# Two attention blocks over 16 images: how queries and keys are stacked and how the row sums become reciprocals

## Chip, cores, metric
One core of one Trainium2 chip. The metric is the device time of the kernel in microseconds, the median of several runs.

## What is computed
Input x is 16 images of 128 channels x 1024 pixels, float32. Each image passes two attention blocks in turn. The reference, cut to what matters:

```python
# block 0: 4 heads of 32 channels
_x = group_norm(x, 32 groups, eps 1e-6) * gn_scale + gn_bias
q, k, v = lin(_x, Wq), lin(_x, Wk), lin(_x, Wv)          # each (16, 4 heads, 32, 1024)
scores  = einsum('bhdxy,bhdij->bhxyij', q, k) / sqrt(128)
weights = softmax(scores, over the 1024 key pixels)
h = lin(einsum('bhxyij,bhdij->bhdxy', weights, v), Wp)
x = (x + h) / sqrt(2)
# block 1: one head of 128 channels
h = group_norm(x, 8 groups, eps 1e-5) * gn_w + gn_b
q, k, v = split(h @ qkv_w.T + qkv_b)
out = softmax(q @ k.T / sqrt(128)) @ v @ proj_w.T + proj_b + x
```

## The kernel before
**Rounds and gaps.** The work on TensorE is written out by hand as tables of pieces. There is a `head`, then 16 rounds (round i is image i's) and a last round that finishes the rest. A round has 64 gaps (`GAPS`), one for each score product of block 0: L828 makes a 128 keys x 512 queries tile of one head, and ScalarE takes its exponential (L553). In the same gap TensorE, ScalarE and VectorE each do the pieces that the tables give for that gap, in the order of the table. A piece is written as (name, argument, image offset, gap on TensorE, gap on ScalarE, gap on VectorE); a gap of 64 or more (`GAPS + n`) is folded into the next round by `folded`. GpSimd and SP don't run by gaps: they have an order of their own and wait on semaphores alone.

**Block 0 in split precision.** q and k are made by `q0` and `k0` (L911). ScalarE writes a rounded high part (`high`, L608), VectorE the rest as a low part (`low`, L702): the tiles q_hi, q_lo, k_hi, k_lo, each 128 channels (4 heads x 32) by 1024 pixels. A score product wants 96 rows to contract for each head: q_stack has hi, lo, hi of the queries in its three groups of 32 partitions, k_stack has hi, hi, lo of the keys. SP makes the stacks: `put_parts` writes the four parts to DRAM (L405), `stack_queries` (L413) and `stack_keys` (L419) read them back with the heads rearranged from partitions to columns. q_stack has three slots of half an image each, k_stack two of a whole image.

**Maxima ahead of the scores.** 64 `max` products for each image (L906, on the same stacks, with VectorE's reduction at L711) find the row maxima for image i+1 during round i. The first and the thirty-third of them wait for the stacks (`stacked_q`, `stacked_k`). A maximum of 16 rows is turned and brought into row 96 of q_stack (`gather`, `shift`, `load_shift` at L425). `MAX_EARLY` and `MAX_LATE` say in which gaps they stand. PSUM has two shared banks for all pieces of this kind, and a third tile, `acc`.

**Sums.** Products with v (`pv`, L846) add into `acc`, whose two halves of an image ScalarE saves to `mix` (`save`). GpSimd adds the probabilities of a half in 14 additions (L517; n counts 28 for a round). `sums` (L929) adds over partitions, ScalarE copies the result to `rb` (L629), where each head's sums stand in all of its 32 partitions. SP then gathers one row of each head into `compact` by four transfers with 32-byte pieces (`turn_sums`, L432), VectorE takes the reciprocal of 64x32 (L735), SP writes it to DRAM (L438), waits, and spreads it to `rb` by four transfers (`spread_reciprocals`, L442). VectorE multiplies `mix` by it (`scale`, L740), and `proj` (L933) follows.

**GpSimd's other work.** `rstd` (L501) for the two norms, after the additions n = 7 and n = 17, and `form_x1` (L506) after n = 21.

**Block 1** runs for image i-1 in eight tiles, eight gaps apart: `score1` (L864 to L866), `max1`, `exp1`, `turn` (L872), `pv1a` and `pv1b` (L885), then `out` (L937). It starts at gap 41 of a round and ends in the next round.

## Time and profile before
| | |
|---|---|
| median of 3 runs | 1848.18 us (1838.9 to 1850.77) |
| the profiled execution | 1824.1 us, its span 1822.1 us |
| TensorE busy | 1641.6 us, 90% |
| VectorE, ScalarE, GpSimd busy | 1133.0, 1076.8, 1096.0 us |
| granted TensorE clock, mean | 0.945 |
| a full round | 105.5 us |

The span runs from the first to the last instruction of the profiled execution. A granted clock of 1.00 is 2.4 GHz and 0.50 is 1.2 GHz.

### The profile page before, as it was taken

What the parts mean: (1) busy time and instruction counts of PE and PEld (TensorE: products, weight loads), DVE (VectorE), ACT (ScalarE), POOL (GpSimd) and SP (SyncE); (2) the same over time, 40 slices, a digit from 0 to 9 for tenths busy, and PEclk for the clock granted to TensorE, in tenths of its full rate; (3) what the DMA queues carried; (4) which work ended last, traced back from release to release, by engine and by line L of the source; (5) the groups of instructions that cost most, each with busy time, mean ns of one, the idle gap of its engine ahead of it and who ended that gap; (6) DMA issues with size and microseconds to landing.
All of it is one profiled execution on the core that took longest, in us unless ns stands there. A gap on an engine that the chain in (4) does not pass through costs nothing.

```text
span 1822.1 us, 25657 instructions
## 1 busy us (share of the span) xinstructions
PE 1641.6 (90%) x9319; PEld 1082.2 (59%) x9319; DVE 1133.0 (62%) x1897; ACT 1076.8 (59%) x1825; POOL 1096.0 (60%) x503
## 2 busy tenths in 40 slices
PE   3889798989989898998989899998989999889978
PEld 1334365656656665665666566665656666556647
DVE  2666575756767675766767566676756666676232
ACT  1245465656656565665656566565656666556734
POOL 1077676665757666575766657477655747765720
PEclk8598899999999999999999999999999999999989
DMA  6131304140321414032140404114040411300000
GB/s 189 58 70 65 76 19 115 38 122 24 100 58 36 117 36 122 24 111 49 35 127 26 122 25 118 46 42 116 25 122 25 124 39 46 101 24 13 13 12 18
DMA packets 65837, 120.63 MB, mean 66 GB/s; under 512 B 26032, under 2 KB 26672, under 8 KB 65712
## 3 DMA queue, kind: packets, MB, share of 16 engines
q1 hardware_dynamic: 65712, 118.99, 23.3%
q8 instruction: 75, 1.23, 0.3%
q14 instruction: 50, 0.41, 0.1%
HBM read 76.22 MB, written 42.21 MB: 65 GB/s over the span
## 4 chain that ended last, share of the span: by engine, by line
PE 72%; DMA 11%; SPq 5%; DVE 5%; issue 3%; ACT 3%; POOL 0%; ACTq 0%; POOLq 0%; DVEq 0%
PE bank L906 13%; PE acc L846 12%; PE scores L885 11%; PE scores L828 10%; DMA k_stack<-parts_dram 9%; PE scores L872 5%; PE acc L911 3%; PE bank L911 3%; PE scores L864 3%; PE scores L865 3%; PE scores L866 3%; DVE halfmax L711 3%; SPq L432 2%; PE bank L933 2%; PE bank L915 2%
## 5 line engine op out<-in xcount | busy, mean ns | idle before, releaser
L517 POOL TENSOR_TENSOR sum<-sum,probs 128x1024 f32<-128x1024 f32 x448 | 1048.7, 2373 | 467.8 <-PE acc L846 425.0
L711 DVE TENSOR_REDUCE halfmax<-bank 128x1 f32<-128x512 f32 x1024 | 679.6, 686 | 363.7 <-PE bank L906 358.1
L553 ACT ACTIVATE probs<-scores 128x512 f32<-128x512 f32 x896 | 519.3, 600 | 458.2 <-PE scores L828 453.5
L906 PE MATMUL bank<-k_stack,q_stack 96*128 96x512 f32 x1024 | 457.3, 465 | 133.1 <-DMA k_stack<-parts_dram 104.7
L828 PE MATMUL scores<-q_stack,k_stack 97*128 97x512 f32 x1024 | 443.9, 446 | 2.3 <-DMA q_stack<-neg 2.3
L906 PEld LDWEIGHTS bank<-k_stack,q_stack 96*128 96x128 f32 x1024 | 198.4, 198 | 302.6 <-issue 179.8
L885 PEld LDWEIGHTS scores<-v,turned 128*128 128x128 f32 x1952 | 253.8, 192 | 36.9 <-ACT turned L573 17.1
L885 PE MATMUL scores<-v,turned 128*128 128x128 f32 x1952 | 260.7, 277 | 4.6 <-ACT turned L573 3.5
L846 PE MATMUL acc<-probs,v 128*32 128x512 f32 x1792 | 236.6, 642 | 0.0
L828 PEld LDWEIGHTS scores<-q_stack,k_stack 97*128 97x128 f32 x1024 | 197.0, 194 | 62.7 <-issue 37.8
L753 DVE TENSOR_REDUCE negmax<-scores 128x1 f32<-128x1024 f32 x128 | 156.5, 1222 | 59.8 <-PE scores L866 59.5
L566 ACT ACTIVATE probs<-scores,negmax 128x1024 f32<-128x1024 f32 x128 | 142.5, 1113 | 24.8 <-DVE negmax L753 24.8
L573 ACT COPY turned<-scores 128x1024 f32<-128x1024 f32 x122 | 123.5, 1012 | 50.3 <-PE scores L872 50.1
L501 POOL TENSOR_TENSOR gn<-gn,minus_half 128x1 f32<-128x1 f32 x32 | 17.6, 550 | 196.7 <-DVE gn L686 196.7
L872 PE MATMUL scores<-consts,probs 128*128 128x128 f32 x1024 | 133.0, 272 | 0.6 <-ACT probs L566 0.4
L872 PEld LDWEIGHTS scores<-consts,probs 128*128 128x128 f32 x1024 | 119.8, 141 | 19.1 <-ACT probs L566 2.0
L846 PEld LDWEIGHTS acc<-probs,v 128*32 128x32 f32 x1792 | 51.1, 116 | 124.5 <-issue 100.1
L553 ACT ACTIVATE sum<-scores 128x512 f32<-128x512 f32 x128 | 73.4, 597 | 76.8 <-PE scores L828 76.7
L864 PE MATMUL scores<-k_hi,q_hi 128*128 128x512 f32 x256 | 107.4, 419 | 3.0 <-DVE k_lo L702 1.8
L865 PE MATMUL scores<-k_lo,q_hi 128*128 128x512 f32 x256 | 104.3, 407 | 0.0
L866 PE MATMUL scores<-k_hi,q_lo 128*128 128x512 f32 x256 | 103.9, 406 | 0.0
L581 ACT ACTIVATE mixed<-scores,rowinv 128x128 f32<-128x128 f32 x128 | 47.1, 368 | 38.0 <-PE scores L885 38.0
(86 smaller groups left out, 1318.9 us busy)
## 6 DMA issues: line engine op xcount, KB each, us to landing
q_stack<-parts_dram SPq DMA_DIRECT2D x96, 256.0 KB, 4.4
k_stack<-parts_dram SPq DMA_DIRECT2D x48, 512.0 KB, 9.4
xin<-x_dram SPq DMA_DIRECT2D x16, 512.0 KB, 3.5
x<-x_dram SPq DMA_DIRECT2D x16, 512.0 KB, 3.6
parts_dram<-q_hi SPq DMA_DIRECT2D x16, 512.0 KB, 2.6
parts_dram<-q_lo SPq DMA_DIRECT2D x16, 512.0 KB, 3.6
parts_dram<-k_hi SPq DMA_DIRECT2D x16, 512.0 KB, 2.6
parts_dram<-k_lo SPq DMA_DIRECT2D x16, 512.0 KB, 3.7
```

The source lines that it names most:

```text
L517: pool.tensor_tensor(total, total, probs[:, ring_slot(i, half, kt), 2 * two:2 * two + 2, :], ALU.add).then_inc(added[two], 1)
L553: act.activation(dst, score_bank(i, index), ACT.Exp).then_inc(exp_done, 1)
L711: dve.tensor_reduce(halfmax[:, h, t, half:half + 1], banks[p][:, :], AX.X, ALU.max).then_inc(bank_free[p][VE], 1)
L753: dve.tensor_reduce(negmax[:, t:t + 1], score1_pair(j, t), AX.X, ALU.max, negate=True).then_inc(negmax_done, 1)
L828: pe.matmul(score_bank(i, index), ks[0:SPLIT + 1, i % 2, h, tile(kt)], qs[0:SPLIT + 1, q_half(i, half), h, :], start=True, stop=True).then ...
L846: mm = pe.matmul(acc[head(h), :], v0[:, i % 2, kt, head(h)], src, start=kt == 0, stop=kt == KT - 1, tile_position=(0, DH * h))
L864: pe.matmul(dst, q_hi[:, tile(t)], k_hi[:, halves(half)], start=True, stop=False)
L865: pe.matmul(dst, q_hi[:, tile(t)], k_lo[:, halves(half)], start=False, stop=False)
L866: pe.matmul(dst, q_lo[:, tile(t)], k_hi[:, halves(half)], start=False, stop=True).then_inc(score1_full, 1)
L872: mm = pe.transpose(score1_pair(j, t)[:, tile(kt)], probs1_of(j, t)[:, tile(kt)], identity)
L885: mm = pe.matmul(out1(j, t), turned_of(j, t)[:, tile(kt)], v1[:, kt, :], start=kt == 0, stop=kt == KT - 1)
L906: mm = pe.matmul(dst[:, :], qs[0:SPLIT, q_half(i, arg // FIRST), h, tile(t % 4)], ks[0:SPLIT, i % 2, h, halves(half)], start=True, stop=True)
```

## The change
1. `put_parts` goes. `stack_queries` copies from the parts in SBUF, for each head and group one transfer of 32 partitions x 512 columns (64 KB), 12 for each half; `stack_keys` likewise, 12 transfers of 32 x 1024 (128 KB). That is 36 transfers an image. They are issued in SP's order where the reading transfers stood; the queries wait for q0 alone, the keys for k0.
2. `turn_sums`, `spread_reciprocals`, `compact` and both DRAM scratch tensors go. VectorE takes the reciprocal of `rb` in place, in four quarters of 128x128 for each half. The multiplication with `mix` goes to GpSimd, after the additions n = 20 (half 0) and n = 2 of the next round (half 1); `form_x1` goes to n = 4, the two `rstd` to n = 6 and n = 20.
3. Pieces stand in other gaps: the first `max` at gap 19 (was 18), the thirty-third at 54 (was 52), the last at 87 as before, with 34 early and 30 late (were 27 and 37); `sums` of half 1 at gap 71 (was 70); the order in which the `max` tiles are taken changes too.

The diff, cut to its core:

```diff
-            ("exp1", t, 0, None, first + 2, None),
+            ("exp1", t, 0, None, first + 1, None),
...
 MAX_EARLY = (
-    18, 24, 26, 28, 29, 30, 31, 32, 33, 35, 49, 50, 51, 51, 52, 54, 56, 57, 58, 61, 62, 65, 66, 67, 68, 78, 87,
+    19, 25, 27, 27, 28, 35, 36, 36, 38, 43, 44, 47, 51, 53, 53, 57, 59, 60, 64, 65, 66, 67, 67, 68, 69, 71, 76, 77,
+    78, 81, 82, 83, 86, 87,
 )
 MAX_LATE = (
-    19, 26, 27, 30, 33, 34, 35, 36, 40, 41, 42, 43, 45, 46, 46, 47, 52, 52, 54, 59, 59, 62, 64, 65, 66, 68, 69, 73,
-    74, 74, 75, 77, 79, 80, 82, 83, 85,
+    19, 24, 25, 28, 29, 30, 31, 31, 33, 34, 41, 44, 45, 47, 48, 50, 51, 54, 55, 59, 60, 62, 62, 67, 68, 69, 73, 73,
+    74, 79,
 )
...
-    ("q0", 0, 2, GAPS + 5, GAPS + 5, GAPS + 6), ("q0", 1, 2, GAPS + 6, GAPS + 6, GAPS + 6),
-    ("k0", 0, 2, GAPS + 6, GAPS + 6, GAPS + 6), ("k0", 1, 2, GAPS + 7, GAPS + 7, GAPS + 7),
-    ("v0", 0, 2, GAPS + 7, GAPS + 8, None), ("v0", 1, 2, GAPS + 16, GAPS + 17, None),
+    ("q0", 0, 2, GAPS + 5, GAPS + 5, GAPS + 5), ("q0", 1, 2, GAPS + 5, GAPS + 5, GAPS + 5),
+    ("k0", 0, 2, GAPS + 6, GAPS + 6, GAPS + 8), ("k0", 1, 2, GAPS + 7, GAPS + 7, GAPS + 8),
+    ("v0", 0, 2, GAPS + 11, GAPS + 11, None), ("v0", 1, 2, GAPS + 20, GAPS + 20, None),
...
-    ("save", 0, 0, None, 35, None), ("sums", 0, 0, 45, 45, None), ("recip", 0, 0, None, None, 51),
-    ("scale", 0, 0, None, None, 59), ("proj", 0, 0, 61, None, 61), ("stats1", 0, 0, None, None, 61),
-    ("save", 1, 0, None, GAPS + 3, None), ("sums", 1, 0, GAPS + 6, GAPS + 6, None),
-    ("recip", 1, 0, None, None, GAPS + 13), ("scale", 1, 0, None, None, GAPS + 19),
-    ("proj", 1, 0, GAPS + 20, None, GAPS + 20), ("stats1", 1, 0, None, None, GAPS + 22),
+    ("save", 0, 0, None, 34, None), ("sums", 0, 0, 45, 45, None), ("recip", (0, 0), 0, None, None, 49),
+    ("recip", (0, 1), 0, None, None, 52), ("recip", (0, 2), 0, None, None, 54), ("recip", (0, 3), 0, None, None, 57),
+    ("proj", 0, 0, 61, None, 61), ("stats1", 0, 0, None, None, 62), ("save", 1, 0, None, GAPS + 2, None),
+    ("sums", 1, 0, GAPS + 7, GAPS + 7, None), ("recip", (1, 0), 0, None, None, GAPS + 10),
+    ("recip", (1, 1), 0, None, None, GAPS + 11), ("recip", (1, 2), 0, None, None, GAPS + 15),
+    ("recip", (1, 3), 0, None, None, GAPS + 15), ("proj", 1, 0, GAPS + 19, None, GAPS + 19),
...
+ADD_THEN = {
+    2: (("scale", 1, -1),), 4: (("form", 0, 0),), 6: (("rstd", 1, -1),), 20: (("rstd", 0, 2), ("scale", 0, 0),),
+}
...
-    ("save", 1, -1, None, 4, None), ("sums", 1, -1, 6, 6, None), ("recip", 1, -1, None, None, 8),
-    ("scale", 1, -1, None, None, 14), ("proj", 1, -1, 15, None, 15), ("stats1", 1, -1, None, None, 15),
+    ("save", 1, -1, None, 4, None), ("sums", 1, -1, 6, 6, None), ("recip", (1, 0), -1, None, None, 7),
+    ("recip", (1, 1), -1, None, None, 7), ("recip", (1, 2), -1, None, None, 7), ("recip", (1, 3), -1, None, None, 7),
+    ("proj", 1, -1, 9, None, 9), ("stats1", 1, -1, None, None, 9),
...
-        STACK_DMAS = 3
+        STACK_DMAS = 3 * HEADS
...
+        def max_of(n):
+            return n // FIRST * 4 + n // 4 % 4, n // 16 % 2, n % 4
...
             def stack_queries(i, half):
-                sp.wait_ge(parts_out, 64 * (i + 1))
+                for piece in [("q0", h, i) for h in range(2)]:
+                    sp.wait_ge(bank_free[bank_of(piece)][VE], given_back(piece))
...
-                for group, k in enumerate((0, 1, 0)):
-                    sp.dma_start(qs[DH * group:DH * (group + 1), q_half(i, half), :, :].bitcast(F32),
-                                 parts_dram[k][:, halves(half)].rearrange("(h r) n -> r h n", h=HEADS)).then_inc(
-                                     stacked_q[half], 16)
+                hi, lo = part[0:2]
+                for h in range(HEADS):
+                    for group, src in enumerate((hi, lo, hi)):
+                        sp.dma_start(qs[DH * group:DH * (group + 1), q_half(i, half), h, :].bitcast(F32),
+                                     src[head(h), halves(half)].bitcast(F32)).then_inc(stacked_q[half], 16)
 
             def stack_keys(i):
-                for group, k in enumerate((2, 2, 3)):
-                    sp.dma_start(ks[DH * group:DH * (group + 1), i % 2, :, :].bitcast(F32),
-                                 parts_dram[k].rearrange("(h r) n -> r h n", h=HEADS)).then_inc(stacked_k, 16)
+                for piece in [("k0", h, i) for h in range(2)]:
+                    sp.wait_ge(bank_free[bank_of(piece)][VE], given_back(piece))
+                hi, lo = part[2:4]
+                for h in range(HEADS):
+                    for group, src in enumerate((hi, hi, lo)):
+                        sp.dma_start(ks[DH * group:DH * (group + 1), i % 2, h, :].bitcast(F32),
+                                     src[head(h), :].bitcast(F32)).then_inc(stacked_k, 16)
...
                 if has0(i + 1):
-                    put_parts(i + 1)
-                if i:
-                    turn_sums(i - 1, 1)
-                if has0(i + 1):
                     stack_queries(i + 1, 0)
                     stack_keys(i + 1)
-                if i:
-                    spread_reciprocals(i - 1, 1)
...
-                turn_sums(i, 0)
-                spread_reciprocals(i, 0)
...
+            def scale(half, i):
+                pool.wait_ge(recip_done, 4 * (2 * i + half + 1))
+                pool.wait_ge(saved, 2 * i + half + 1)
+                pool.tensor_tensor(mix[:, halves(half)], mix[:, halves(half)], rb[:, halves(half)],
+                                   ALU.mult).then_inc(scaled, 1)
...
-            def recip(half, i):
-                dve.wait_ge(sums_in, 16 * HEADS * (2 * i + half + 1))
-                dve.reciprocal(compact[:, half, :], compact[:, half, :]).then_inc(recip_done, 1)
...
+            def recip(half, quarter, i):
+                if quarter == 0:
+                    piece = ("sums", half, i)
+                    dve.wait_ge(bank_free[bank_of(piece)][SC], given_back(piece))
+                cut = rb[:, HALF * half + C * quarter:HALF * half + C * (quarter + 1)]
+                dve.reciprocal(cut, cut).then_inc(recip_done, 1)
```

## Rows read from the trace of the kernel before

**Rows 1.** The page, part 1: busy us, share and instructions of each engine.
```profile
PE 1641.6 (90%) x9319; PEld 1082.2 (59%) x9319; DVE 1133.0 (62%) x1897; ACT 1076.8 (59%) x1825; POOL 1096.0 (60%) x503
```

**Rows 2.** Waits, whole span: who waited for whom, us in total, times, longest.
```profile
PE bank L906 <- DMA k_stack<-parts_dram: 104.7, 16, 15.2
```

**Rows 3.** Timeline of TensorE: start, us, what, count, [idle before <-releaser].
```profile
43.08 1.19 PE L906 MATMUL bank<-k_stack,q_stack 96*128 96x512 f32 x2 [15.20 <-DMA k_stack<-parts_dram]
...
104.70 1.19 PE L906 MATMUL bank<-k_stack,q_stack 96*128 96x512 f32 x2 [3.62 <-DMA k_stack<-parts_dram]
...
713.43 0.39 PE L866 MATMUL scores<-k_hi,q_lo 128*128 128x512 f32 x1
713.66 0.39 PE L828 MATMUL scores<-q_stack,k_stack 97*128 97x512 f32 x1
719.74 0.76 PE L906 MATMUL bank<-k_stack,q_stack 96*128 96x512 f32 x1 [5.69 <-DMA k_stack<-parts_dram]
...
782.67 0.27 PE L924 MATMUL bank<-consts,rowmax 128*16 128x128 f32 x1
...
800.70 1.06 PE L929 MATMUL bank<-sum,ones 128*32 128x512 f32 x8
```

**Rows 4.** Windows: length, busy us of each engine, granted clock, DMA share, GB/s.
```profile
700.00:705.00 5.00, 5.00 (x34) 3.56 (x36) 3.02 (x4) 3.65 (x7) 0.00 (x0) 1.00 0.96 383
...
710.00:714.00 4.00, 4.00 (x27) 3.30 (x25) 2.13 (x3) 2.40 (x5) 4.00 (x2) 1.00 1.05 222
714.10:719.70 5.60, 0.00 (x0) 0.00 (x0) 0.00 (x0) 0.63 (x2) 5.60 (x4) 0.80 0.79 153
719.70:726.00 6.30, 6.26 (x25) 2.98 (x26) 4.87 (x4) 1.69 (x3) 4.16 (x2) 0.64 0.23 83
...
705.50:811.00 105.50, 99.00 (x586) 67.13 (x582) 70.49 (x119) 67.27 (x115) 68.06 (x32) 0.97 0.26 71
```

**Rows 5.** Timeline of SP's queue: start of the issues, us, count.
```profile
23.00 0.33 SPq L405 DMA_DIRECT2D parts_dram<-q_hi  x1
...
698.88 0.33 SPq L405 DMA_DIRECT2D parts_dram<-q_hi  x1
...
702.58 3.34 SPq L432 DMA_DIRECT2D compact<-rb  x4
706.01 1.48 SPq L413 DMA_DIRECT2D q_stack<-parts_dram  x3
...
719.79 1.71 SPq L442 DMA_DIRECT2D rb<-recip_dram  x4
...
1744.28 2.40 SPq L432 DMA_DIRECT2D compact<-rb  x4
```

**Rows 6.** DMA issues: count, KB each, median us from issue to landing.
```profile
k_stack<-parts_dram SPq DMA_DIRECT2D x48, 512.0 KB, 9.4
...
rb<-recip_dram SPq DMA_DIRECT2D x128, 64.0 KB, 2.0
```

**Rows 7.** Groups of instructions: busy us, mean ns | idle before, releaser.
```profile
L517 POOL TENSOR_TENSOR sum<-sum,probs 128x1024 f32<-128x1024 f32 x448 | 1048.7, 2373 | 467.8 <-PE acc L846 425.0 <-ACT probs L553 42.8
...
L740 DVE TENSOR_TENSOR mix<-mix,rb 128x512 f32<-128x512 f32 x32 | 64.9, 2027 | 5.2 <-DMA rb<-recip_dram 5.2
...
L758 DVE RECIPROCAL rowinv<-rowsum 128x1 f32<-128x1 f32 x128 | 19.7, 154 | 23.8 <-ACT probs L566 23.8
...
L735 DVE RECIPROCAL compact<-compact 64x32 f32<-64x32 f32 x32 | 10.8, 339 | 5.2 <-DMA compact<-rb 5.1
```

**Rows 8.** Timeline of GpSimd in one round.
```profile
705.25 16.26 POOL L517 TENSOR_TENSOR sum<-sum,probs 128x1024 f32<-128x1024 f32 x7 [10.21 <-PE acc L846]
...
761.59 9.36 POOL L517 TENSOR_TENSOR sum<-sum,probs 128x1024 f32<-128x1024 f32 x4 [13.98 <-PE acc L846]
...
786.48 14.07 POOL L517 TENSOR_TENSOR sum<-sum,probs 128x1024 f32<-128x1024 f32 x6
```

**Rows 9.** Timeline of the tail, VectorE's multiplication.
```profile
1754.20 0.68 DVE L740 TENSOR_TENSOR mix<-mix,rb 128x512 f32<-128x512 f32 x1
```

More of the change, by code:

```diff
@@ L64 @@
 BLOCK1 = [(p[0], p[1], -1) + p[3:] for t in range(KT) for p in tile_pieces(t, TILE_FIRST + TILE_GAPS * t)] + [
-    ("out", 0, -1, GAPS + 14, None, GAPS + 14), ("out", 1, -1, GAPS + 41, None, GAPS + 41),
+    ("out", 0, -1, GAPS + 13, None, GAPS + 13), ("out", 1, -1, GAPS + 42, None, GAPS + 43),
 ]
@@ L274, in bass_two_attention_blocks @@
         rb = sb("rb", [C, N])
-        compact = sb("compact", [C // 2, 2, HEADS * KT])
         halfmax = sb("halfmax", [C, HEADS, KT, 2])
@@ L426, in load_shift @@
                     "p h (t n) -> p (h t) n", n=C).bitcast(F32), neg[:, :].bitcast(F32)).then_inc(shift_loaded, 16)
-            def turn_sums(i, half):
-                piece = ("sums", half, i)
-                sp.wait_ge(bank_free[bank_of(piece)][SC], given_back(piece))
-                for h in range(HEADS):
-                    sp.dma_start(compact[:, half, KT * h:KT * (h + 1)], rb[DH * h:DH * h + 1, halves(half)].rearrange(
-                        "o (p e) -> o p e", e=KT)).then_inc(sums_in, 16)
-            def spread_reciprocals(i, half):
-                n = 2 * i + half + 1
-                sp.wait_ge(recip_done, n)
-                sp.dma_start(recip_dram[:, halves(half)].rearrange("h (p e) -> p h e", e=KT),
-                             compact[:, half, :].rearrange("p (h e) -> p h e", h=HEADS)).then_inc(recip_out, 16)
-                sp.wait_ge(recip_out, 16 * n)
-                for h in range(HEADS):
-                    sp.dma_start(rb[head(h), halves(half)],
-                                 recip_dram[h:h + 1, halves(half)].to_broadcast([DH, HALF])).then_inc(rb_loaded, 16)
             def store(i, half):
@@ L527, in _ @@
                     add(i, half, kt, two)
-                    if n == 7 and has0(i - 1):
-                        rstd(1, i - 1)
-                    if n == 17 and has0(i + 2):
-                        rstd(0, i + 2)
-                    if n == 21:
-                        form_x1(i)
+                    for piece, arg, offset in ADD_THEN.get(n, ()):
+                        if has0(i + offset):
+                            if piece == "form":
+                                form_x1(i + offset)
+                            elif piece == "scale":
+                                scale(arg, i + offset)
+                            else:
+                                rstd(arg, i + offset)
+            scale(1, images - 1)
             rstd(1, images - 1)
@@ L708, in maximum @@
                 p = bank_of(piece)
-                t, half, h = n // 8, n // 4 % 2, n % 4
+                t, half, h = max_of(n)
                 dve.wait_ge(bank_full[p], filled(piece))
@@ L731, in shift @@
                                   ALU.mult).then_inc(bank_free[p][VE], 1)
-            def recip(half, i):
-                dve.wait_ge(sums_in, 16 * HEADS * (2 * i + half + 1))
-                dve.reciprocal(compact[:, half, :], compact[:, half, :]).then_inc(recip_done, 1)
-            def scale(half, i):
-                dve.wait_ge(rb_loaded, 16 * HEADS * (2 * i + half + 1))
-                dve.wait_ge(saved, 2 * i + half + 1)
-                dve.tensor_tensor(mix[:, halves(half)], mix[:, halves(half)], rb[:, halves(half)],
-                                  ALU.mult).then_inc(scaled, 1)
+            def recip(half, quarter, i):
[4 more added lines that the diff above has]
+                dve.reciprocal(cut, cut).then_inc(recip_done, 1)
             def residual(half, i):
@@ L804, in _ @@
                         elif name == "recip":
-                            recip(arg, img)
-                        elif name == "scale":
-                            scale(arg, img)
+                            recip(*arg, img)
                         elif name == "proj":
@@ L901, in work @@
                 if name == "max":
-                    t, half, h = arg // 8, arg // 4 % 2, arg % 4
+                    t, half, h = max_of(arg)
                     if arg % FIRST == 0:
```

34 lines of the change are left out of this document (10 added, 24 removed).

## Prediction
> **What bounds the kernel now.** I began with the page: TensorE is busy for 1641.6 us, 90% of the span, and VectorE, ScalarE and GpSimd for 59 to 62% [rows 1]. The list of waits then says what ends TensorE's idle time. Inside the rounds it is almost one thing: the `max` product of L906 waits for the stacked keys, 104.7 us in 16 waits, of which the longest (15.2 us) is in the head [rows 2]. The timeline of one round shows the place: TensorE runs the score product of gap 17 and then that of gap 18 at 713.66, and stands until 719.74 [rows 3]. The windows give the price. In 714.1 to 719.7 TensorE does nothing, in 719.7 to 726.0 the granted clock is 0.64 on average (it has fallen to the lower of the two levels, 1.2 GHz, after the idle stretch, and comes back to 2.4 GHz), and of the round's 105.5 us 99.0 are busy [rows 4]. So a round is TensorE's work plus one stall. The stall costs 85.9/14 = 6.1 us by the waits (104.7 less 15.2 and less the 3.6 of the first round [rows 2, 3]) and 6.3 x (1 - 0.64) = 2.3 us of half-speed work: 8.4 us.
>
> Where the keys' time goes is seen on SP's queue [rows 5]: q's parts leave for DRAM at 698.88; at 702.58 four `compact` transfers of the reciprocals take 3.34 us of issue; three query transfers go at 706.01 and take 1.48 us of issue, the three of keys follow and land 9.4 us (median) after their issue [rows 6], the last just before 719.74.
>
> **Removed: the trip through DRAM.** In place of four transfers out, six in and the four `compact` ones between, SP issues 12 for the first half of the queries as soon as both q_lo are there (the 698.88 of today; their new places are at most a gap earlier, which I keep as reserve), then 12 for the keys. Issue: three neighbours took 1.48 us, 0.49 each; four 64 KB ones to 32 partitions took 1.71 us, 0.43 each [rows 5]. 24 x 0.49 = 11.8, so the last is issued by 710.7, and at 2.0 us to landing for a 64 KB one [rows 6] it lands at 712.7. Data: 12 x 64 KB and 12 x 128 KB. When the six DRAM-fed transfers to 32-partition groups ran, the engines were full (share 1.05) at 222 GB/s [rows 4]. At that rate the queries (0.79 MB, 3.5 us) are bound by issue, 5.9 us to 704.8, and the keys (1.57 MB) by data, 7.1 us, landing at 704.8 + 7.1 + 2.0 = 713.9. No SBUF to SBUF transfer of this size is in the trace. One end is 712.7; the other is the worst run of issues from SBUF to SBUF, 3.34/4 = 0.835 us: 698.9 + 20.0 + 2.0 = 720.9. I take 713.9, since both the 64 KB row and the 222 GB/s row have the new destination shape, while the 0.835 is of 32-byte pieces that also waited in a full queue.
>
> The Trainium skill has a rule against this edit: "DMA: Bandwidth & Descriptors", section Rules for kernel authors, says to coalesce many small transfers, and its section Bandwidth gives 138 GB/s at 64 KB; as an estimate by that figure 2.36 MB need 17.1 us, keys would land near 718, and 3 us of stall would stay. Its rule that 32 partitions reach 8 of 16 ports, some 218 GB/s ("SBUF — State Buffer", Door 1), agrees with the 222 measured [rows 4].
>
> **Moved: the first `max`**, from gap 18 to 19. TensorE reaches it after gap 18's score and its three L864 to L866 products. Today's gap 18 score ends at 714.05; the products stand 0.23 us apart [rows 3], so four more slots give 715.0. The rest of the stretch between k0 and this point keeps its load: 9 `max` products before and after, v0's first half moves in and its second out. 713.9 is before 715.0: no stall, and with no idle stretch no fallen clock. The margin is 1.1 us, so I charge 0.5 us per round. What is late next is TensorE's own work: 97.1 us of a round (99.0 - 2.3, and 0.4 of small waits).
> Gain: 14 x 8.4 = 117.6; the first round has 3.6 + 2.3 = 5.9 [rows 3]; less 14 x 0.5 = 7.
>
> The second half's queries are issued when score 31 is read; the first `max` that wants them is at gap 54 (52 before), twenty gaps later. 12 issues (5.9 us) there hide, and the shift's transfer ahead of them stays ahead. In that stretch the queue loses five reciprocal transfers and four spreads, so `load_shift` and the stores come no later.
>
> **Head.** Today q_lo is there at 23.00 [rows 5] and the first `max` runs at 43.08 [rows 3]. The same sum gives 23.0 + 5.9 + 7.1 + 2.0 = 38.0. What follows is paced by VectorE, so 5.1 us are gained whole.
>
> **Reciprocals.** Each half now costs VectorE four of 128x128. 128x1 takes 154 ns, 64x32 339 ns: 6.0 ns an element, 154 + 127 x 6.0 = 0.91 us [rows 7]; lower end 0.34 us (the 64x32 row itself, as if the width cost nothing), upper 1.36 (that row scaled in full, 4 x 0.339). I take 0.91, by rows of the same operation. Eight make 7.3 us a round. Out go two multiplications at 2.03 and two 64x32 at 0.34, 4.7 us. VectorE goes from 70.5 us of 105.5 [rows 4] to 73 of 97.5, still below TensorE. Behind each 0.91 queue `max` reductions whose banks TensorE wants; two banks cover most. Cost between 0 and 2.5 us a round, taken 0.3, 5 us in all.
>
> **Multiplication on GpSimd.** 128x1024 takes 2.37 us [rows 7], half of it 1.2. Today's multiplication on VectorE, two operands in SBUF, takes 2.03 us on average [rows 7]. GpSimd's place is at issue, not its load (68 of 105.5 us [rows 4]). For half 0 it sits after add 20: adds start at 761.59 [rows 8] (seven by 778.2), `rstd` to about 778.8, then it waits for the fourth reciprocal of gap 57, over at some 783.5 (the shift product of gap 58 was at 782.67 [rows 3]), and ends at 784.7. Seven more adds (16.6) end at 801.3. Today they end at 786.48 + 14.07 = 800.55 [rows 8] and the sums are made at 800.70 [rows 3], no slack at all; the sums move to gap 7, behind one more L885 group, at about 803.6. Slack 2.3 us. `form_x1` leaves this chain. For half 1, the adds start at 705.25 [rows 8], three end at 712.4, and the fourth reciprocal (gap 15) by about 713; 1.2 us more is before gap 19. Cost 0, and above zero only past these slacks.
>
> **Tail.** From the first `compact` transfer at 1744.28 [rows 5] to the multiplication at 1754.20 and its 0.68 [rows 9] are 10.6 us; four reciprocals and 1.2 are 4.9. TensorE fills part of this with tiles: 3 us of the 5.7, bounds 0 and 5.7.
>
> **Sum.** 117.6 + 5.9 + 5.1 + 3.0 - 7 - 5 = 119.6. The profiled execution took 1824.1 us, so 1704.5 after. The median of the runs, 1848.18, is 24.1 above it; I add the same: 1729.
>
> **Rivals.** (a) Part of the stall stays, because SBUF to SBUF is slower than the 222 GB/s. For it: no row of this shape, thin margin, the 0.835 us of issue in one run. Against: 383 GB/s were moved at 700 to 705 with SBUF as the source, on the wide shape [rows 4]. A stall of 2 to 4 us with part of the clock's loss is 3 us a round: 1729 + 42 = 1771. (b) GpSimd or VectorE becomes late: the fourth reciprocal or the product over 2.3 us later than I put it, and the sums wait; 2.5 us a round, 16 rounds: 1769. (c) The new way is no shorter: 0.83 us a transfer, keys at 720.9, stall 5.9 as now; the head loses what the tail gains: 1845. (d) Slower: SP's queue becomes the bound. From 0.85 us a transfer on, the 24 take more than the DRAM way; at 1.0 us the keys land at 724.9, stall 9.9 against 6.1, 14 x 3.8 = 53, the head 6 later: about 1905. Only a queue that blocks would do so; the 3.34 us run shows that it can for a moment [rows 5].
>
> **Chances.** Forecast 0.65 (1703 to 1750), (a) 0.18, (b) 0.09, (c) 0.03, (d) 0.05. A change under 1% is about what a measurement can't tell from none. Faster by over 1% (below 1829.7) are the forecast, (a) and (b), 0.92; same 0.03; slower 0.05. The low end is all gains without the charges (132 us: 1716) less the spread of the runs below their median (9 us) and some us for the blocked multiplications that go: 1703. The high end takes in (a) past its middle, and (b): 1775.
>
> **What would show it.** `max` waits of TensorE for the stack near zero, rounds near 97.5 us, granted clock above 0.98 in the rounds; SP's issues 0.45 to 0.5 us apart, keys landing before gap 19's product; reciprocals at 0.9 us; GpSimd's product at 1.2 us, TensorE not waiting at the sums. I am wrong if issues stand 0.8 us apart, if the keys' data come under 180 GB/s, or if the `proj` or sums products begin to wait.

## The result, and the profile of the changed kernel

The changed kernel takes 1686.55 us (median of 4 runs, 1684.23 to 1687.4); the kernel before took 1844.65 us beside it (4 runs, 1838.9 to 1850.77). The ratio is 0.914, 95% interval 0.9105 to 0.9176. That is 42 us below the forecast of 1729 and 16 us below the low end of the range. The profiled execution took 1684.23 us, its span 1682.3 us.

The page, part 1 (compare [rows 1]):
```profile
PE 1601.9 (95%) x9319; PEld 1065.3 (63%) x9319; DVE 1161.5 (69%) x1961; ACT 1069.0 (64%) x1825; POOL 1130.1 (67%) x535
```

TensorE's list of waits (us in total, times, longest), the answer to [rows 2]:
```profile
PE bank L886 <- DMA k_stack<-k_lo: 15.4, 3, 12.3
PE bank L886 <- DVE halfmax L696: 11.7, 38, 1.4
...
PE bank L909 <- POOL sum L499: 6.1, 1, 6.1
PE bank L913 <- POOL mix L488: 5.0, 1, 5.0
```

The 16 waits for the stacked keys have become 3: the head's 12.3 us, and 0.7 and 2.4 us in the first two rounds (at 98.65 and 178.98). From the third round on there is none. TensorE's timeline, in the head and in one round, stands against [rows 3]:
```profile
40.51 1.19 PE L886 MATMUL bank<-k_stack,q_stack 96*128 96x512 f32 x2 [12.32 <-DMA k_stack<-k_lo]
...
759.13 0.39 PE L808 MATMUL scores<-q_stack,k_stack 97*128 97x512 f32 x1
759.36 0.65 PE L886 MATMUL bank<-k_stack,q_stack 96*128 96x512 f32 x2
```

The first `max` (759.36) follows the score product of gap 19 with no idle time before it. The windows, a full round first (compare the last row of [rows 4]), then the stretch in which the stacks are sent and the few us behind it. The columns are as in [rows 4]:
```profile
732.00:829.00 97.00, 96.56 (x584) 66.02 (x583) 72.33 (x123) 66.77 (x115) 70.22 (x34) 1.00 0.20 50
741.00:757.20 16.20, 15.92 (x98) 10.69 (x97) 12.02 (x18) 10.26 (x19) 7.29 (x4) 1.00 0.58 131
757.20:761.00 3.80, 3.80 (x24) 2.25 (x27) 3.30 (x5) 1.97 (x4) 3.80 (x3) 1.00 0.50 138
```

TensorE is busy for 96.56 of 97.00 us and its granted clock is 1.00 throughout: 2.4 GHz. The rounds were forecast at 97.1 us of TensorE's work, and the measured round is 97.0.

SP's queue (compare [rows 5]): the `xin` load ahead of them, the first and the last issue of the 24, and the one that stood longer:
```profile
732.31 0.34 SPq L402 DMA_DIRECT2D xin<-x_dram  x1
...
740.87 0.51 SPq L414 DMA_DIRECT2D q_stack<-q_hi  x1
...
742.05 1.23 SPq L414 DMA_DIRECT2D q_stack<-q_hi  x2
...
751.60 1.77 SPq L423 DMA_DIRECT2D k_stack<-k_lo  x1
...
756.58 0.59 SPq L423 DMA_DIRECT2D k_stack<-k_lo  x1
```

The pair at 742.05 takes 1.23 us of issue, and with the gaps between them one direct transfer follows the other after 0.63 us (twelve take 7.6). One of the keys' stood 1.2 us longer here. The whole queue has 13 such places, where an issue stands 0.7 to 1.3 us longer: 8 of them ahead of the keys' end, 5 among the second half's queries. The parts of the page on DMA issues and on groups (columns as in [rows 6] and [rows 7]):
```profile
q_stack<-q_hi SPq DMA_DIRECT2D x256, 64.0 KB, 2.0
k_stack<-k_hi SPq DMA_DIRECT2D x128, 128.0 KB, 2.4
...
L723 DVE RECIPROCAL rb<-rb 128x128 f32<-128x128 f32 x128 | 117.9, 934 | 3.2 <-ACT rb L614 3.2
L488 POOL TENSOR_TENSOR mix<-mix,rb 128x512 f32<-128x512 f32 x32 | 41.1, 1283 | 58.9 <-DVE rb L723 58.9
```

So the last key transfer, issued at 756.58, lands at about 759.0 (by the median of 2.4 us), and TensorE wants it at 759.36. The margin is about 0.4 us, and some 1.5 in a round where no issue stands.

**Where the 139.8 us went, profile against profile** (spans 1822.1 and 1682.3). SP issues one `xin` load in each round, which makes a ruler; the first, at 0.73, is mark zero. Mark three stands at 162.26 before and 153.91 after: 8.4 us in the head and the first round. From there to mark fifteen twelve rounds take 1265.64 us before (to 1427.90) and 1160.72 after (to 1314.63): 104.9 us, 8.74 a round. From there to the end it is 394.2 against 367.7: 26.5 us. The same stretches in the forecast are 10.2 (5.1 + 5.9 less one round's charges of 0.8), 91.2 (12 x 7.6) and 18.2 (2 x 7.6 + 3).

### The profile page after: what moved, and what is told of

Its sections match the earlier page's. It is cut to its first block, busy times and chain, and to the rows that moved or that the text cites. A ratio compares the mean times of both kernels' runs of the same rounds, so it can differ in the third digit from the quotient of the medians.

```text
span 1682.3 us, 25820 instructions
## 1 busy us (share of the span) xinstructions
PE 1601.9 (95%) x9319; PEld 1065.3 (63%) x9319; DVE 1161.5 (69%) x1961; ACT 1069.0 (64%) x1825; POOL 1130.1 (67%) x535
## 3 DMA queue, kind: packets, MB, share of 16 engines
q1 hardware_dynamic: 38320, 76.53, 17.7%
## 4 chain that ended last, share of the span: by engine, by line
PE 88%; DVE 5%; SPq 2%; ACT 2%; issue 1%; DMA 1%; POOL 0%; ACTq 0%; POOLq 0%
PE bank L886 15%; PE acc L826 14%; PE scores L865 14%; PE scores L808 13%; PE scores L852 7%; PE scores L844 4%; PE scores L845 3%; PE scores L846 3%; PE bank L895 3%; PE bank L891 3%; PE acc L891 3%; DVE halfmax L696 3%; PE bank L913 2%; PE bank L909 2%; SPq L414 1%
## 5 line engine op out<-in xcount | busy, mean ns | idle before, releaser
L886 PE MATMUL bank<-k_stack,q_stack 96*128 96x512 f32 x1024 | 444.6, 454 | 34.1 <-DMA k_stack<-k_lo 15.4
L826 PE MATMUL acc<-probs,v 128*32 128x512 f32 x1792 | 222.4, 608 | 0.0
L723 DVE RECIPROCAL rb<-rb 128x128 f32<-128x128 f32 x128 | 117.9, 934 | 3.2 <-ACT rb L614 3.2
L844 PE MATMUL scores<-k_hi,q_hi 128*128 128x512 f32 x256 | 104.7, 409 | 1.8 <-DVE k_lo L687 1.8
L488 POOL TENSOR_TENSOR mix<-mix,rb 128x512 f32<-128x512 f32 x32 | 41.1, 1283 | 58.9 <-DVE rb L723 58.9
```

The lines of the kernel that those rows point to most:

```text
L826: mm = pe.matmul(acc[head(h), :], v0[:, i % 2, kt, head(h)], src, start=kt == 0, stop=kt == KT - 1, tile_position=(0, DH * h))
L844: pe.matmul(dst, q_hi[:, tile(t)], k_hi[:, halves(half)], start=True, stop=False)
L886: mm = pe.matmul(dst[:, :], qs[0:SPLIT, q_half(i, arg // FIRST), h, tile(t % 4)], ks[0:SPLIT, i % 2, h, halves(half)], start=True, stop=True)
```

## Experiments

Theory I: SP issues one direct transfer every 0.63 us whatever its size, so the keys' landing is set by the count of issues ahead of them and by the place of q0. The stall with its clock is what the stacks give back. Theory P: a multiplication on VectorE with two operands in SBUF is held off while GpSimd adds back to back, so the dense new places pay only if the two don't meet. Theory D, against it: the trip through DRAM varies from execution to execution. The other rivals were: the data rate sets the landing; the places are worth little; VectorE has no room; the old profile is a fair one.

**1. The old kernel traced again, unchanged.**

> The kernel before, unchanged, executed and traced once more. Its profiled execution took 1824.1 us, its other runs 1838.9 to 1850.8, while those of the changed kernel lie within 3 us of their profile. Theory P (VectorE's multiplication of two SBUF operands, L740, is held off by GpSimd's additions): the trace of before has one L740 of 10.5 us, behind four additions, with TensorE idle 8.3 us; this execution, if it is slower, shows more of them, some 8 to 10 us for each, and they account for the difference in span. Theory D (the trip through DRAM varies): the 14 waits for the stacked keys are longer than the 6.1 us of the first trace and account for it, while the long L740 stay at one. Theory C: the granted clock is lower at the same waits.

Measured: 1842.52 us (10 runs, 1838.02 to 1845.48), ratio 0.9991 [0.9974, 1.0007]; its profiled span is 1841.6 us, against 1822.1 of the profile that the prediction read. In 19 runs of the kernel before beside it none was under 1837.33, and the lowest in all later experiments was 1833.76. So the profiled execution of 1824.1 us was a rare one, and the 24.1 us between it and the median belong to that execution. The marks say where the 19.5 us between the two spans are: 2.3 to mark three (164.56), 6.7 in the twelve rounds, 10.5 behind them. A part of the last has a name. VectorE's multiplications behind the last mark in this trace:
```profile
1638.72 10.52 DVE L740 TENSOR_TENSOR mix<-mix,rb 128x512 f32<-128x512 f32 x1
...
1683.25 8.79 DVE L740 TENSOR_TENSOR mix<-mix,rb 128x512 f32<-128x512 f32 x1
```
and GpSimd beside them:
```profile
1637.07 11.62 POOL L517 TENSOR_TENSOR sum<-sum,probs 128x1024 f32<-128x1024 f32 x5
...
1672.86 18.63 POOL L517 TENSOR_TENSOR sum<-sum,probs 128x1024 f32<-128x1024 f32 x8 [13.98 <-PE acc L846]
```
An operation that takes 0.68 us alone [rows 9] takes 10.52, and both long ones end 0.55 us after GpSimd's series ends (1649.24 against 1648.69; 1692.04 against 1691.49). The first profile has one such operation, and behind it the one that took 8.79 above:
```profile
1629.08 10.50 DVE L740 TENSOR_TENSOR mix<-mix,rb 128x512 f32<-128x512 f32 x1
...
1673.64 1.87 DVE L740 TENSOR_TENSOR mix<-mix,rb 128x512 f32<-128x512 f32 x1
```
The end of the long one is 1639.58, and GpSimd's five additions from 1627.44 ended at 1639.04. TensorE's longest wait for `halfmax` in that trace is 8.3 us, and it stands there. The other got in between two additions, and the addition behind it took 2.82 us in place of 2.35; in the second trace the same operation waited for four additions, and TensorE for it, 6.8 us. So the same multiplication, started 1.0 us into the same addition, once gets its turn at the next boundary and once three additions later, and a part of what made the first execution quick is that it got in. The mean of 2027 ns in [rows 7] hides this: it is that of a group which goes from 0.68 to 10.50. Of the 6.7 us in the rounds, 3.0 are longer waits for the keys (107.7 us in all against 104.7), which is theory D's term; the rest was not traced.

**2. The old kernel with the multiplication on GpSimd.**

```diff
-            dve.tensor_tensor(mix[...], mix[...], rb[...], ALU.mult)   # at gaps 59 and GAPS + 19
+            pool.tensor_tensor(mix[...], mix[...], rb[...], ALU.mult)  # after additions 20 and 7
+    form_x1 after addition 4, rstd(1) after addition 8
```

> Before, with the multiplication by the reciprocals on GpSimd (after additions n = 7 and n = 20; rstd of block 1 after n = 8, form_x1 after n = 4); stacks and reciprocals still go through DRAM. Theory P: nothing is left that holds VectorE up, so all runs lie within 3 us of the profile, and the time is 1824 less 8 to 12: 1810 to 1816 us, a ratio of 0.980 to 0.986. Theory D: the spread of the runs stays at 10 us and the median is 1830 to 1838.

Measured: 1834.33 us (10 runs, 1829.37 to 1841.25), ratio 0.9956 [0.9937, 0.9975]. This is theory D's forecast and not P's: the median is in D's 1830 to 1838 and the runs still spread by 12 us. Without any multiplication on VectorE the waits for the keys are 115.6 us in this trace, against 104.7 and 107.7 in the two of the kernel before. What is gained is 8 us, and it lies behind mark fifteen (396.0 us against 404.7 in experiment 1); the rounds are no shorter (106.5 us against 106.0). In the rounds of the kernel before the multiplication has at most one addition to wait for: it takes 1.3 us in the first half and up to 2.7 in the second.

**3. The changed kernel with the multiplication back on VectorE.**

```diff
+    ("scale", 0, 0, None, None, 59), ... ("scale", 1, 0, None, None, GAPS + 16)
-            pool.tensor_tensor(mix[...], mix[...], rb[...], ALU.mult)
+            dve.tensor_tensor(mix[...], mix[...], rb[...], ALU.mult)
```

> The changed kernel with the multiplication back on VectorE, at gaps 59 and 80; direct stacks and reciprocals in place stay. Theory P: multiplications of 0.7 to 2.7 us and, in some places, of 7 us and more behind a row of additions, each with a TensorE wait of 5 to 10 us; 1690 to 1715 us, with runs spread by 5 us or more. Theory D: no more than 3 us above the changed kernel (1686.6), and its small spread.

Measured: 1872.51 us (1867.39 to 1880.85), ratio 1.0163 [1.0122, 1.0203]: 1.6% slower than the kernel before, and 186 us slower than the changed one, where theory P had put 4 to 28. The multiplications of the trace (ns, least, median, greatest), and VectorE's timeline in two rounds:
```profile
L721 DVE TENSOR_TENSOR mix<-mix,rb x32: 691/5830/12208, 146.6 to 1793.6; 128x512 f32<-128x512 f32 x32
...
407.00 2.16 DVE L721 TENSOR_TENSOR mix<-mix,rb 128x512 f32<-128x512 f32 x1
...
731.89 4.46 DVE L721 TENSOR_TENSOR mix<-mix,rb 128x512 f32<-128x512 f32 x1
...
801.33 7.18 DVE L721 TENSOR_TENSOR mix<-mix,rb 128x512 f32<-128x512 f32 x1
```
GpSimd's in the later of the two:
```profile
724.10 11.69 POOL L495 TENSOR_TENSOR sum<-sum,probs 128x1024 f32<-128x1024 f32 x5 [17.61 <-PE acc L827]
735.79 1.55 POOL L484 TENSOR_SCALAR x<-x,proj_bias 128x1024 f32<-128x1024 f32 x1
...
796.30 11.66 POOL L495 TENSOR_TENSOR sum<-sum,probs 128x1024 f32<-128x1024 f32 x5
```
TensorE's waits:
```profile
PE bank L887 <- DVE halfmax L689: 122.3, 63, 8.6
PE bank L887 <- DMA k_stack<-k_lo: 15.5, 3, 11.4
```
Again the multiplications end some 0.55 us after a GpSimd addition does (736.35 against 735.79; 808.51 against 807.96). All 16 of the first half wait for two boundaries between additions or more, up to five, and end where the series stops. Of the 15 of the second half that meet additions, 7 wait through one boundary and get in where `form_x1` (L484) follows, and 8 get in at the first boundary between two additions, as the one at 407.00: the addition behind it takes 2.81 us in place of 2.35. The 4.46 us of 731.89 and the 2.16 us of 407.00 both start 0.8 us into the same addition of their rounds; what decides between them no run shows. Behind the multiplications queue the `max` reductions, and TensorE waits for their banks 122 us; the keys are not the cause, their waits are as in the changed kernel. But this alone doesn't exclude that VectorE's queue is simply too full for two more operations. Hence:

**4. The same, but GpSimd rests while VectorE multiplies; and the same again, earlier.**

```diff
+                    if n == 2 and has0(i - 1):
+                        pool.wait_ge(scaled, 2 * (i - 1) + 2)
+                    if n == 20:
+                        pool.wait_ge(scaled, 2 * i + 1)
```

> The kernel after with the multiplication on VectorE in gaps 59 and 80 (64 + 16), as in e4_mul_on_dve, and one thing more: GpSimd waits for its end before addition 3 and before addition 21, so that it adds nothing while VectorE multiplies. Theory I (the multiplication is held off by GpSimd's back-to-back additions, and this is all of the 186 us that e4 lost): the multiplications take 0.7 to 1.3 us instead of a median of 5.8, TensorE's waits for halfmax fall from 122 us to under 20, and the kernel comes to 1690 to 1715 us; what is above 1686.5 is GpSimd's later sums. Rival R (VectorE has no room for two more operations in these places, its queue is simply late): the multiplications are short, but the waits for halfmax stay above 60 us and the time above 1780.

> As e10_mul_while_idle, with the multiplications right behind the fourth reciprocal (gaps 57 and 79), so that GpSimd gets on 1.5 to 3 us sooner. Theory I: as e10 or up to 15 us faster, 1686 to 1710; if e10 is slow only because sums are late, here is where it is made good. Rival R: as e10, above 1780, since VectorE's work is the same.

Measured: 1687.13 us (1685.57 to 1688.12), ratio 0.9175 [0.9133, 0.9218], and 1687.11 us (1685.95 to 1688.17), ratio 0.9177. Both equal the changed kernel. In the first, the tile `mix` on VectorE (duration in ns, least, median, greatest):
```profile
L725 DVE TENSOR_TENSOR mix<-mix,rb x32: 668/681/1182, 147.6 to 1613.2; 128x512 f32<-128x512 f32 x32
```
TensorE's waits in it:
```profile
PE bank L891 <- DMA k_stack<-k_lo: 14.7, 3, 11.3
PE bank L891 <- DVE halfmax L693: 11.3, 37, 1.4
```
The same operation at the same gaps on the same engine, now 0.68 us (one of the 32 takes 1.18); the 122 us of waits are 11, and all 185 us are back. That the additions hold the multiplication off, and that this is the whole loss of experiment 3, is shown, and rival R has fallen: VectorE has room. Here which engine multiplies makes no difference; that GpSimd isn't adding at that moment makes all of it. GpSimd's rests cost nothing that can be measured (rounds are 97.0 and 97.2 us).

**5. The old kernel with the direct stacks alone** (queries, then `compact`, then keys in SP's order).

```diff
-                    put_parts(i + 1)
+                    stack_queries(i + 1, 0)   # 12 transfers from the parts in SBUF
                 turn_sums(i - 1, 1)
-                    stack_queries(i + 1, 0)
-                    stack_keys(i + 1)
+                    stack_keys(i + 1)         # 12 transfers from the parts in SBUF
```

> The kernel before with one part of the change alone: the 36 direct transfers. Reciprocals through DRAM, the multiplication on VectorE and all places stay; the four compact transfers of the sums stand between those of the queries and those of the keys. By the issue price of the prediction (0.49 us) the keys would land at 698.9 + 5.9 + 2.6 + 5.9 + 2.4 = 715.7 and the stall would be 1.6 us in place of 6.1: about 85 us faster than before. By the price seen in the changed kernel (0.633 us): 698.9 + 7.6 + 2.6 + 7.6 + 2.4 = 719.1, a stall of 5 us, a round all but the same: 5 to 25 us faster, ratio 0.986 to 0.997.

Measured: 1809.26 us (1803.78 to 1809.93), ratio 0.9823 [0.9796, 0.9851]; rounds of 103.8 us. TensorE's waits, and windows: a stall, and the work right after it.
```profile
PE bank L902 <- DMA k_stack<-k_lo: 48.1, 15, 11.8
PE bank L933 <- DVE halfmax L707: 21.4, 13, 2.2
...
703.35:706.22 2.87, 0.01 (x1) 0.03 (x1) 0.00 (x0) 0.69 (x2) 2.87 (x2) 1.00 0.76 160
706.22:709.00 2.78, 2.78 (x10) 1.58 (x14) 1.91 (x3) 0.36 (x1) 2.78 (x2) 0.61 0.33 86
```
The keys' wait falls from 6.1 to 36.3/14 = 2.6 us a round, and 1.6 of that comes back as waits of the `proj` product for `halfmax`: TensorE gets there sooner, and VectorE doesn't. The gain of 31 us is above the 5 to 25 expected by the dearer issues, and far under the 85 by the cheaper.

**6. The changed kernel with the stacks through DRAM.**

```diff
+                    put_parts(i + 1)
                     stack_queries(i + 1, 0)   # 3 transfers each, from parts_dram
```

> The changed kernel with the stacks through DRAM again and everything else kept. k_lo is there 5.6 us after q_lo in the new places; two parts go out (0.8 us and 3.6 to land), six transfers of 1.48 + 1.4 us of issue come back and the keys land 9.4 us after: 19.2 us after k_lo... as numbers of the changed kernel's round, 746.4 + 0.8 + 3.6 + 2.9 + 9.4 = 763.1 against TensorE's arrival at 759.6: a stall of 3.5 us and 1 to 2 us of lower clock, 14 x 5 = 70: 1740 to 1770 us. If the clutter of the compact transfers had been most of the old stall, it would stay under 1705 us.

Measured: 1813.21 us (1810.4 to 1814.8), ratio 0.9842 [0.9817, 0.9867]:
```profile
PE bank L892 <- DMA k_stack<-parts_dram: 104.7, 16, 15.5
```
The wait is back to what it was before [rows 2] (that it is so to the tenth is chance: other executions have 107.7 and 115.6), although the `compact` transfers that the prediction blamed for part of it are gone and the first `max` is a gap later; I had expected a smaller stall. SP's queue says why, in a round of this run:
```profile
702.72 0.43 SPq L413 DMA_DIRECT2D parts_dram<-k_lo  x1
707.00 1.27 SPq L421 DMA_DIRECT2D q_stack<-parts_dram  x3
```
The reading transfers leave 4.3 us after the last part does, for they wait for its landing (4.2 us, median). In the old round the same wait was from 702.10 to 706.01, and the `compact` transfers stood inside it [rows 5]: they held nothing up. Together, 5 and 6 make a square: stacks alone give 31 us, all else alone 27, both 154. The parts are worth more than twice as much together as apart.

**7. The changed kernel with each key transfer cut in two.** The same bytes, 12 issues more.

```diff
+                        for cut in range(2):
-                            ks[..., h, :] <- src[head(h), :]
+                            ks[..., h, halves(cut)] <- src[head(h), halves(cut)]
```

> The changed kernel with each of the 12 key transfers cut into two of 64 KB: 36 issues in place of 24 ahead of the first max. If issue sets the landing (0.633 us each), the last lands 12 x 0.633 = 7.6 us later, less the margin of 0.6 us: a stall of 7 us and 2 us of lower clock a round, 15 x 9 = 135, head 7.6: some 1825 us (1790 to 1840). If data set it (1.57 MB in the same time), nothing changes: within 10 us of 1686.6.

Measured: 1821.44 us (1820.05 to 1822.24), ratio 0.9887 [0.9864, 0.9911]; rounds 105.9. TensorE's timeline and two windows, stall and aftermath:
```profile
727.73 1.19 PE L888 MATMUL bank<-k_stack,q_stack 96*128 96x512 f32 x2 [6.74 <-DMA k_stack<-k_lo]
...
720.99:727.73 6.74, 0.01 (x1) 0.03 (x1) 1.04 (x1) 1.69 (x3) 6.74 (x5) 0.83 0.48 123
727.73:734.00 6.27, 6.27 (x24) 2.05 (x25) 1.72 (x3) 0.00 (x0) 2.32 (x2) 0.63 0.04 14
```
Twelve issues are 12 x 0.63 = 7.6 us; less the margin of 0.4, and less 0.4 since a 64 KB one lands after 2.0 us and not 2.4 [rows 6], 6.8 us of stall are to be expected, and the timeline has 6.74. The issues set the landing, not the data: the spacing of the 64 KB key transfers is again 0.63 us, and the DMA share in the stall is 0.48.

**8. The changed kernel with the old places** (tables of `max` and of the pieces up to q0, k0, v0 as before the change).

```diff
-    19, 25, 27, 27, 28, 35, ...           # MAX_EARLY, MAX_LATE, order of the tiles, NEXT0
+    18, 24, 26, 28, 29, 30, ...
```

> The changed kernel with the old places of the maxima (first at gap 18), their old order, and the old gaps of q0, k0 and v0. Issue of one of the 24 transfers takes 0.633 us in the changed kernel's trace and not 0.49: the keys then land 15.2 + 2.4 = 17.6 us after q_lo, and in the old places TensorE comes for them 15.2 us after it. Theory I (issue sets the landing): a stall of 2 to 3 us a round for the keys, with little or no fall of the clock: 14 x 2.5 = 35, some 1720 us (1705 to 1740). Rival (the places don't matter once DRAM is out): within 5 us of the changed kernel.

Measured: 1751.34 us (1748.04 to 1752.53), ratio 0.9498 [0.9473, 0.9523]; rounds of some 101.2 us, 4.2 more than in the changed kernel. I had put the places at less. TensorE's waits:
```profile
PE bank L885 <- DMA k_stack<-k_lo: 28.5, 16, 12.2
PE bank L885 <- DVE halfmax L695: 18.8, 53, 1.1
...
PE bank L885 <- ACT rb L613: 7.4, 14, 0.5
PE scores L864 <- ACT turned L557: 6.9, 17, 0.6
```
It is no single wait. Some 1.1 us a round are the keys again; the rest of what the list shows is many waits of at most 1.1 us behind VectorE and ScalarE, and those for `rb` (7.4 us) don't occur in the changed kernel.

**9. The changed kernel with only q0's second piece a gap later.**

```diff
-    ("q0", 0, 2, GAPS + 5, GAPS + 5, GAPS + 5), ("q0", 1, 2, GAPS + 5, GAPS + 5, GAPS + 5),
+    ("q0", 0, 2, GAPS + 5, GAPS + 5, GAPS + 6), ("q0", 1, 2, GAPS + 6, GAPS + 6, GAPS + 6),
```

> The kernel after with the second product of q0 and the first VectorE pass of q0 one gap later (gap 6, as before the change; a gap is about 1.5 us), all other places unchanged. Theory I (24 issues of 0.63 us end only 0.6 us before the first max wants the keys, and the earlier place of q0 is what made room): SP's first query transfer starts 0.8 to 1.5 us later, the stack waits of TensorE go from 15.4 us in 3 to 18 to 30 us in some 16, and the kernel takes 1693 to 1710 us. Rival Q (the place of q0 is of no account, the keys have room): within 3 us of 1686.5, 3 waits.

Measured: 1698.76 us (1697.12 to 1700.09), ratio 0.924 [0.9205, 0.9275]. TensorE's waits, one of them on its timeline, and the windows of a round with the wait and of one without:
```profile
PE bank L886 <- DMA k_stack<-k_lo: 22.8, 11, 12.0
...
768.57 0.70 PE L886 MATMUL bank<-k_stack,q_stack 96*128 96x512 f32 x2 [1.09 <-DMA k_stack<-k_lo]
...
740.26:838.58 98.32, 96.79 (x584) 66.03 (x583) 72.36 (x123) 66.73 (x115) 70.25 (x34) 1.00 0.19 49
838.58:935.74 97.16, 96.73 (x584) 66.01 (x583) 72.26 (x123) 66.66 (x115) 70.16 (x34) 1.00 0.19 50
```
Twelve us for one piece in one gap: the first query transfer leaves 9.92 us after the mark in place of 8.56, 1.36 us later. In a round where an issue ahead of the keys' end stands longer (2.44 us for two at 761.50 in the first of the two windows), the keys are 1.1 to 1.2 us late and the round takes 98.3 us; where none does (838.58), there is no wait and the round takes 97.16. So the margin is 0.2 to 0.4 us in the one kind of round, and the new place of q0 is what pays for the dearer issues. Of the 12 us 4.0 are in the first round (mark two to mark three), where the granted clock of TensorE was 0.86 against 0.94.

**10. Head and tail of the changed kernel.** The keys of image 0 issued by ScalarE beside SP's queries, and the last half's sums for blocks 5 to 7 made by TensorE in place of GpSimd.

```diff
+                    if (kind, gap) == ("head", 10):
+                        act.dma_start(ks[...], src[head(h), :])   # 12 of them
...
+BY_POOL = 4   # blocks above it: pe.matmul(dst, ones, probs[...]) in the sums of the last half
```

> The changed kernel with two repairs outside the rounds. Head: the 12 key transfers of image 0 are issued by ScalarE beside SP's 12 of the queries. Tail: of the last half's additions GpSimd makes those of kt 1 to 4, and TensorE takes the blocks 5 to 7 into the sums product, so the sums don't wait for six additions of 2.35 us. By the issue price the head's first max comes 7 us earlier (33.5 in place of 40.5), and the rest of the head follows; in the tail the 6.1 us wait goes and the product is 3 us longer, while its chain starts 8 to 12 us earlier: 4 to 8 us. In all 10 to 15 us: 1672 to 1677 us, ratio to before about 0.908. If the head is held by the row of maxima from its image's queries on SP or by the tail's tiles in order, under 4 us.

Measured: 1685.49 us (1685.32 to 1686.28), ratio 0.9151 [0.9129, 0.9173]: no difference from the changed kernel, against some 10 to 14 us expected. The head's wait falls from 12.3 to 10.6 us only. In the tail the wait for the sums goes and the one for `mix` stays. TensorE's waits, and two windows of the head, with both queues at work (ScalarE's last key issue is at 33.73) and after it:
```profile
PE bank L896 <- DMA k_stack<-k_lo: 13.8, 4, 10.6
...
PE bank L927 <- POOL mix L488: 5.2, 1, 5.2
...
28.00:34.30 6.30, 0.27 (x2) 0.18 (x2) 0.16 (x1) 0.00 (x0) 0.56 (x1) 0.62 1.03 239
34.30:38.85 4.55, 0.00 (x0) 0.03 (x1) 0.00 (x0) 0.00 (x0) 0.00 (x0) 0.50 1.07 235
```
Here is the limit that the prediction had put on the single queue. Two queues issue twice as fast (each still one in some 0.63 us), the engines are full at 235 to 239 GB/s, near the 222 of [rows 4], and a key transfer of ScalarE's queue lands after 3.8 us (median) in place of 2.4. What goes out beside the keys from 29.54 on are the second half's queries, which SP sends until 37.80; the first `max` comes at 38.85 in place of 40.51, 1.7 us earlier and not 7. In the tail GpSimd's product is waited for as before (5.2 us), and the end doesn't come sooner.

## Why the prediction was wrong

The direction, the main mechanism (the stall for the keys and its fallen clock go) and the length of the new round were right; the time was 42 us too high, and 16 us outside the range. Two steps of the sum were at fault: the offset from profile to median, and the price of the multiplication on VectorE. By the prediction's own steps:

**Sum: the offset of 24.1 us.** This is the step that failed most. It carried the distance between the profiled execution and the median over to the new kernel. The changed kernel's profiled run is 2.3 us below its median; 21.8 us of the 42 are this. The distance was that of one lucky execution, which the range of the runs (1838.9 at the lowest, with the profile at 1824.1) already hinted at; a second trace of the same kernel has a span of 1841.6 in place of 1822.1 (experiment 1).

**Removed: the trip through DRAM.** 14 x 8.4 us was put right: 8.74 a round were found. That the stall goes whole was partly luck, for both terms beneath it were off and cancelled. The issue costs 0.63 us, not 0.49, so 24 take 15.2 us and not 11.8, and 1.2 more where one stands: the last is issued 15.7 us after the first. Data bound nothing: the 222 GB/s row that I took for the keys was not the limit (131 to 138 GB/s and a DMA share of 0.50 to 0.58 while they run); one queue didn't reach it, two did (experiment 10). So two of the prediction's signs came out against it, issues 0.45 to 0.5 us apart and, among those of being wrong, data under 180 GB/s, and still there was no stall. Against the dearer issues stands q0's place, which I "kept as reserve": from the first query transfer to the first `max` are 18.5 us (740.87 to 759.36), not the 16.1 of my sum (698.9 to 715.0). Experiments 7 and 9 show both halves of that. The four `compact` transfers, which the prediction removed with the trip, had cost the keys nothing (experiment 6). The charge of 0.5 us a round (7 us) for the thin margin wasn't needed: from the third round on there is no such wait.

The rule on coalescing in "DMA: Bandwidth & Descriptors", section Rules for kernel authors, of the Trainium skill points the right way: experiment 7 has the same bytes in 12 more transfers and gives the stall back whole. My estimate by that page's 138 GB/s, 17.1 us and 2.0 to landing, came near the 18.1 measured (740.87 to 759.0) by chance, for the time goes by the count and not by bytes: 64 KB and 128 KB transfers are issued at the same 0.63 us.

**Reciprocals.** Estimated 0.91 us each, measured 0.934. The charge of 0.3 us a round (5 us) was not needed: with VectorE busy for 72.3 us in 97, TensorE's waits for `halfmax` are 11.7 us in the whole kernel, against 17.7 before (8.3 of them the one wait below).

**Multiplication on GpSimd.** Estimated 1.2 us and no cost: measured 1.28 us, and no wait of TensorE in the rounds. What I missed is what it removes, and this is the second step that failed. I costed the one on VectorE at its mean of 2.03 us. One of them took 10.5 us in the profile that I read and held TensorE for 8.3. That is the size of the excess of the last stretch, 26.5 us against 18.2, where the smaller terms cancel (charges not needed, better rounds, less from the tail). I gave it "some us" in the low end only. In "SBUF — State Buffer", section Who interferes with whom, the Trainium skill says that a VectorE instruction with two SBUF inputs contends with a GpSimd instruction that reads SBUF, and one with at most one SBUF input doesn't. The traces agree: the reciprocals (894 to 953 ns, all 128) and the reductions (626 to 694 ns, all 1024) of the changed kernel keep their durations beside the same additions, the multiplication doesn't. In these traces it waits often for several additions and not for one, up to six in experiment 3, and sometimes gets in between two.

**Head and tail.** Head: first `max` at 40.51, forecast 38.0; 2.6 us of 5.1, since 24 issues at 0.63 are 3.4 us more than at 0.49. Tail: forecast 3 us. Less the two stalls and the held multiplication next to nothing is left (26.5 - 2 x 8.74 - 8.3 = 0.7): TensorE waits there for GpSimd's last sums (6.1, as before with 6.4) and now for its product (5.0).

Put together: 4.1 (rounds better than 8.4) + 9.6 (charges, 12 rounds) + 8.3 (last stretch) - 1.9 (head) = 20.1, and 21.8 for the offset: 42. No rival came in. A late VectorE, as in (b), is what experiment 3 makes of this kernel, though by the blocked multiplication, which (b) doesn't name; and (a) is what experiment 9 shows in small.

**Left open.** Why the old kernel's rounds differ by half a us between two executions is only partly traced (3.0 of 6.7 us), and with it why the first execution was so quick. What lets a waiting multiplication in between two additions in one round and not in another isn't known. How the 65 us of the new places divide among their pieces was tried for q0 alone (12 us).

## What to carry to other kernels

Before adding the distance between a profile and the median to a forecast, ask whose it is: a profile that lies below every timed run may be a lucky execution, as here, and then the new kernel doesn't inherit the distance. Read the least, median and greatest duration of a group, not its mean: one operation of 0.68 us that once takes 10.5 names a contention, and then it can be enough, as in experiment 4, to keep the two engines apart at that moment by a wait on the one that has slack. When a large transfer becomes many small ones, count the issues between the producer and the first reader, and buy room by moving the producer's last piece: here one gap for one piece was worth 12 us. The parts of such a change don't add up: the direct stacks in the old places, with the other engines not replanned, gave 31 of the 154 us.

## What the runs showed of the hardware that was not expected

- A VectorE multiplication with both operands in SBUF that meets a back-to-back series of GpSimd additions is held off, often for several of them: up to 10.5 us for 0.68 us of work, and 12.2 us in experiment 3. It ends some 0.55 us after one of the additions does (1639.58 and 1639.04, 1649.24 and 1648.69, 1692.04 and 1691.49, 808.51 and 807.96 at the end of a series). It isn't shut out for the whole series: 8 of 31 in experiment 3 got in between the first two additions that they met, the addition behind then took 2.8 us in place of 2.35, and 7 more where GpSimd went over to `form_x1`.
- A direct transfer from SBUF to SBUF with 32 partitions costs SP's queue 0.63 us, for 64 KB and 128 KB alike, and one in most rounds stands 0.7 to 1.3 us longer (751.60, 1.77 us in place of 0.59). While one queue sent these the core's engines moved 131 to 138 GB/s; with two it was 235 to 239, at a share of 1.03 to 1.07. The transfers from DRAM took 0.49 and 0.43 us [rows 5].
- What a stall costs beyond itself: after 1.1 us idle the granted clock stayed at 1.00 (experiment 9). After 2.9 us (ten rounds of experiment 5) it was 0.50 to 0.77 over the next 2.8 us in seven of them and 1.00 in three, as at 602.55. After 5.7 [rows 4] and 6.7 us (experiment 7) it was 0.63 to 0.64 over the next 6.3. So in these traces the short waits were cheaper, us for us, than the long ones.
